# Sixteen frequency groups in place of seventeen, and the loops of two stages written out

## What is computed

```python
def _stu_conv(phi, u, n):            # n = 8192, phi: (sl, 16), u: (b, sl, d)
    Vf = jnp.fft.rfft(phi, n=n, axis=0)
    Uf_p = jnp.fft.rfft(u, n=n, axis=1)
    Uf_m = jnp.fft.rfft(u * sgn3, n=n, axis=1)
    U_plus = irfft(Vf[None, :, :, None] * Uf_p[:, :, None, :], n=n, axis=1)[:, :sl]
    U_minus = irfft(Vf[None, :, :, None] * Uf_m[:, :, None, :], n=n, axis=1)[:, :sl]
    return (U_plus, U_minus * sgn)
...
out = einsum('btkd,k,kde->bte', U_plus, s, Mpp) + einsum('btkd,k,kde->bte', U_minus, s, Mpm)
```

## Time and profile before

| what | value |
|---|---|
| median of 3 runs | 3113.92 us (3101.46 to 3119.89) |
| profiled execution, its own time | 3099.33 us |
| its span, first to last instruction | 3097.6 us |
| TensorE busy / VectorE busy / ScalarE busy | 2450.0 / 1541.0 / 1359.1 us |
| mean granted TensorE clock | 0.897 of full speed |
| `spectrum`: first matmul of line 856 to the first load of `inverse` | 938.4 to 2280.0 us |
| `inverse`: its first to its last matmul | 2286.0 to 2419.7 us |

### The profile page before, as it was taken

How to read it: one execution, slowest core, us unless ns; L and a number is a source line. 1 busy time by engine, 2 the same in 40 slices (tenths; PEclk the granted TensorE clock), 3 DMA queues, 4 the chain that set the end, 5 groups by cost and what they waited for, 6 DMA issues and landing times. The chain is left out here.

```text
span 3097.6 us, 87088 instructions
## 1 busy us (share of the span) xinstructions
PE 2450.0 (79%) x36136; PEld 1874.9 (61%) x36136; DVE 1541.0 (50%) x3563; ACT 1359.1 (44%) x2720; POOL 314.7 (10%) x607
## 2 busy tenths in 40 slices
PE   0455998544609999998999898999979697599998
PEld 0334888522208888888888887888843463144444
DVE  6441343333505656465555555656621165277777
ACT  0562344255006556565656565656621076133332
POOL 0102111100020000000000000000012100122221
PEclk9765899777859999999999999999989698699999
DMA  6437555432461111111111111111048740000000
GB/s 200 128 97 122 104 104 104 118 120 106 139 135 34 43 41 42 42 42 42 42 42 42 42 42 40 44 37 47 22 145 294 260 128 15 12 23 22 23 22 28
DMA packets 189077, 242.74 MB, mean 78 GB/s; under 512 B 36891, under 2 KB 147278, under 8 KB 185146
## 3 DMA queue, kind: packets, MB, share of 16 engines
q1 hardware_dynamic: 154325, 124.05, 15.0%
q0 software_dynamic: 30368, 94.52, 11.3%
q10 hardware_dynamic: 3969, 18.31, 1.5%
HBM read 145.54 MB, written 91.27 MB: 76 GB/s over the span
## 5 line engine op out<-in xcount | busy, mean ns | idle before, releaser
L958 DVE COPY spc_g<-spc_pz 128x512 f32<-128x512 f32 x1088 | 670.4, 683 | 457.3 <-PE spc_pz L856 457.1
L936 ACT ACTIVATE spc_g<-spc_pz 128x512 f32<-128x512 f32 x1088 | 587.6, 610 | 353.4 <-PE spc_pz L856 351.2
L856 PE MATMUL spc_pz<-spc_v,spc_as 108*128 108x128 bf16 x8704 | 604.5, 223 | 46.8 <-issue 32.9
L856 PEld LDWEIGHTS spc_pz<-spc_v,spc_as 108*128 108x128 bf16 x8704 | 519.8, 99 | 141.6 <-issue 51.7
L874 PE MATMUL spc_pz<-spc_g,spc_u 128*20 128x128 f32 x17408 | 499.6, 274 | 27.8 <-DVE spc_g L958 18.3
L874 PEld LDWEIGHTS spc_pz<-spc_g,spc_u 128*20 128x20 f32 x17408 | 479.7, 133 | 56.9 <-ACT spc_g L936 41.3
L841 PE MATMUL spc_pu<-spc_f,spc_s 128*128 128x256 f32 x816 | 223.7, 400 | 71.8 <-DMA spc_s<-s_sf 71.8
L1470 PE MATMUL moe_ex<-moe_ew,moe_d 128*128 128x512 f32 x512 | 249.8, 610 | 33.0 <-DVE moe_yt L1627 32.6
L1627 DVE SCALAR_TENSOR_TENSOR moe_yt<-moe_ex,moe_gb,moe_yt 128x128 f32<-128x128 f32 x768 | 209.6, 344 | 103.3 <-ACT moe_yt L1529 101.0
L505 DVE SCALAR_TENSOR_TENSOR inv_xo<-inv_pa,inv_mask,inv_xo 128x256 f32<-128x256 f32 x256 | 123.6, 484 | 222.3 <-PE inv_pa L463 161.2
L483 ACT ACTIVATE inv_b<-inv_pb 112x1024 f32<-112x1024 f32 x128 | 125.1, 1021 | 222.0 <-PE inv_pb L442 222.0
(11 more groups left out here) (199 smaller groups left out, 2214.7 us busy)
## 6 DMA issues: line engine op xcount, KB each, us to landing
s_yd<-spc_yo SPq DMA_DIRECT2D x136, 160.0 KB
spc_s<-s_sf POOLq DMA_DIRECT2D x36, 512.0 KB, 6.6
ivs_y<-s_yd POOLq DMA_DIRECT2D x34, 512.0 KB, 5.1
s_td<-ivs_to SPq DMA_DIRECT2D x34, 512.0 KB, 4.7
s_sf<-fwd_so ACTq DMA_DIRECT2D x16, 1024.0 KB, 4.7
ln_t<-s_td SPq DMA_DIRECT2D x32, 512.0 KB, 3.7
inv_x<-s_xn SPq DMA_DIRECT2D x88, 112.0 KB
inv_x<-s_xn POOLq DMA_DIRECT2D x88, 112.0 KB, 8.0
```

Of the source, the lines that this page charges most:

```text
L856: m = pe.matmul(pz[:, (p + 2) % 3, e // 4, 2 * FT * (e % 4):2 * FT * (e % 4) + 2 * FT], AS[:, x, 8 * p + e, :], V[:, k, x, :, FT * t:FT * ...
L936: act.activation(g_out(p, 0), g_in(p, 0), ACT.Copy).then_inc(ga, 1)
L958: v.tensor_copy(g_out(p, 1), g_in(p, 1)).then_inc(gd, 1)
```

## The change

NF1 becomes 16. The real group 16 is packed into group 0: group 0 now has f = 32 f2 for f2 below 64 and f = 16 + 32 (f2 - 64) for the others, so that its real input is slot 0 and its "imaginary" one slot 16. The tables `fw` and `fi` have zeros where the two don't mix. The table `fi` gets a fourth slice, as both halves of the output now have weights of their own. Frequency 0 shares its place with frequency 2048, both real numbers; they must not be mixed as a complex product, so VectorE makes a small tile `U0` (memset and four copies of 128x8) at the start of `spectrum`, and `make_y` takes it for that one frequency. The loops of `spectrum` and `inverse` are written out in Python, so no register, no dynamic address and no branch is left in them. The zero rows in DRAM go.

```diff
-NF1, NF2, NA = 17, 128, 16
+NF1, NF2, NA = 16, 128, 16
...
-            for b in range(NB):
-                sp.dma_start(S["SF"][b, 32], zero[:, 0:256]).then_inc(out_done, 16)
-                n += 1
-            sp.dma_start(S["SP"][32], zero[:, 0:2 * KX]).then_inc(out_done, 16)
...
+        def f_loop(body):
+            for f in range(NF1):
+                body(f, f % 2, f == NF1 - 1)
...
-            with sp.Fori(0, NF1 // 2) as i:
-                for k in range(2):
-                    f = 2 * i + k
-
-                    sp.wait_ge(u_done, UB * (f + 1))
-                    load_tokens((f + 2) % NF1, k)
-                    sp.wait_ge(g_done, NPR * NUN * (f + 1))
-                    load_filters((f + 2) % NF1, k)
...
+            for f in range(NF1 - 2):
+                sp.wait_ge(u_done, UB * (f + 1))
+                load_tokens(f + 2, f % 2)
+                sp.wait_ge(g_done, NPR * NUN * (f + 1))
+                load_filters(f + 2, f % 2)
...
+                    if f == 0:
+                        pe.wait_ge(u0_ready, 5)
...
-                                w = U[:, k, s0:s0 + 5, :, FT * t + 4 * g + j].rearrange("d s b -> d (s b)")
+                                w = U[:, k, s0:s0 + 5, :, FT * t + 4 * g + j] if f + t + g + j else U0[:, x, c]
+                                w = w.rearrange("d s b -> d (s b)")
...
-            with pe.Fori(0, NF1 // 2) as i:
-                for k in range(2):
-                    body(2 * i + k, k, i, False)
-            body(NF1 - 1, 0, NF1 // 2, True)
+            f_loop(body)
...
         def _(v):
+            v.memset(U0[:], 0.0).then_inc(u0_ready, 1)
+            v.wait_ge(u0_ready, 1)
+            v.wait_ge(u_ready, UB + 2)
+            for x in range(2):
+                for c in range(2):
+                    s0 = 3 * c + 4 - x
+                    v.tensor_copy(U0[:, x, c, 3 * c:3 * c + 2], U[:, 0, s0:s0 + 2, :, 0]).then_inc(u0_ready, 1)
...
-        F = A.sb("f", [P, 2, 3, P])
+        F = A.sb("f", [P, 2, 4, P])
...
         def f_loop(eng, body):
-            with eng.Fori(0, NF1 // 2) as i:
-                for k in range(2):
-                    body(2 * i + k, k, i)
-            body(NF1 - 1, 0, NF1 // 2)
...
+            for f in range(NF1):
+                body(f, f % 2, f // 2)
...
-                        for part, w in enumerate(((0, 2), (1, 0))[c]):
-                            m = pe.matmul(pt[:, k, c, CH * x:CH * x + CH], F[:, k, w, :], Y[:, k, part, x, :],
+                        for part in range(2):
+                            m = pe.matmul(pt[:, k, c, CH * x:CH * x + CH], F[:, k, 2 * c + part, :], Y[:, k, part, x, :],
```

More of the change, by code:

```diff
@@ L881, in _, with body @@
             pe.wait_ge(as_in, 16 * 12)
-            def body(f, k, i, last):
-                pe.wait_ge(in_v[k], 96 * (f // 2) + 96 if isinstance(f, int) else 96 * i + 96)
+            def body(f, k, last):
+                pe.wait_ge(in_v[k], 96 * (f // 2) + 96)
                 if not last:
-                    pe.wait_ge(in_s[1 - k], 48 * i + 48 + 48 * k)
+                    pe.wait_ge(in_s[1 - k], 48 * ((f + 1) // 2) + 48)
                 for t in range(NTL):
@@ L945, in body @@
                                 act.activation(yo[:, t, 4 * h:4 * h + 4, :].rearrange("p g e -> p (g e)"), y_at(h), ACT.Copy).then_inc(ya, 1)
-            f_loop(act, body)
+            f_loop(body)
         @block.vector
         def _(v):
+            v.memset(U0[:], 0.0).then_inc(u0_ready, 1)
[5 more added lines that the diff above has]
+                    v.tensor_copy(U0[:, x, c, 3 * c:3 * c + 2], U[:, 0, s0:s0 + 2, :, 0]).then_inc(u0_ready, 1)
             def body(f, k, last):
@@ L964, in body @@
                                 v.tensor_tensor(y, y_at(h), y, ALU.add).then_inc(yd, 1)
-            f_loop(v, body)
+            f_loop(body)
         @block.sync
@@ L975, in body @@
                     for j in range(4):
-                        sp.dma_start(one(dst[:, t, j], f), yo[32 * j:32 * j + YR, t]).then_inc(y_out[t], 16)
-            f_loop(sp, body)
+                        sp.dma_start(dst[f, t, j], yo[32 * j:32 * j + YR, t]).then_inc(y_out[t], 16)
+            f_loop(body)
             for t in range(NTL):
@@ L995, in f_loop @@
         def f_loop(eng, body):
-            with eng.Fori(0, NF1 // 2) as i:
-                for k in range(2):
-                    body(2 * i + k, k, i)
-            body(NF1 - 1, 0, NF1 // 2)
-        def at(ap, f):
-            return ap[f] if isinstance(f, int) else ap[bass.ds(f, 1)].rearrange("o p m -> (o p) m")
+            for f in range(NF1):
+                body(f, f % 2, f // 2)
         @block.gpsimd
@@ L1009, in body @@
                     src = S["YD"][:, :, 3 * NB * part:3 * NB * part + 2 * NB].rearrange("f p r e -> f p (r e)")
-                    pool.dma_start(Y[:, k, part].rearrange("p x m -> p (x m)"), at(src, f)).then_inc(loads[k], 16)
-                pool.dma_start(F[:, k].rearrange("p s b -> p (s b)"), at(I["fi"], f)).then_inc(loads[k], 16)
+                    pool.dma_start(Y[:, k, part].rearrange("p x m -> p (x m)"), src[f]).then_inc(loads[k], 16)
+                pool.dma_start(F[:, k].rearrange("p s b -> p (s b)"), I["fi"][f]).then_inc(loads[k], 16)
             f_loop(pool, body)
@@ L1679, in tables @@
         d1[:, k, 1, 1:, k] = -np.sin(th[:, 1:16])
-    b, f2 = np.arange(P), np.arange(NF2)
+    b = np.arange(P)
     fw = np.zeros((NF1, P, 2, 4, NF2))
-    fi = np.zeros((NF1, NF2, 3, P))
+    fi = np.zeros((NF1, NF2, 4, P))
+    f2 = np.arange(NF2)
     for f1 in range(NF1):
         f = f1 + 32 * f2
+        if f1 == 0:
+            f[64:] -= 2048 - 16
         for z in range(2):
@@ L1687, in tables @@
             c, s = np.cos(t), np.sin(t)
-            fw[f1, :, 0, 2 * z:2 * z + 2] = np.stack([c, -s], 1)
-            if f1 not in (0, 16):
+            if f1:
+                fw[f1, :, 0, 2 * z:2 * z + 2] = np.stack([c, -s], 1)
                 fw[f1, :, 1, 2 * z:2 * z + 2] = np.stack([s, c], 1)
+            else:
+                s[:, 0] = -np.cos(np.pi * (b + z))
+                fw[0, :, 0, 2 * z:2 * z + 2, 0:64] = np.stack([c, -s], 1)[:, :, 0:64]
+                fw[0, :, 1, 2 * z:2 * z + 2, 64:] = np.stack([c, -s], 1)[:, :, 64:]
         t = 2 * np.pi * (np.outer(f, b) % 4096) / 4096
-        w = (1.0 if f1 in (0, 16) else 2.0) / 4096
-        fi[f1] = np.stack([np.cos(t), np.sin(t), -np.sin(t)], 1) * w
+        c, s = np.cos(t) * 2 / 4096, np.sin(t) * 2 / 4096
+        if f1:
+            fi[f1] = np.stack([c, -s, s, c], 1)
+        else:
+            c[0], s[0] = 1 / 4096, -np.cos(np.pi * b) / 4096
+            fi[0, 0:64, 0:2] = np.stack([c, -s], 1)[0:64]
+            fi[0, 64:, 2:4] = np.stack([c, -s], 1)[64:]
     d2 = np.zeros((32, 4, NA, 4))
```

29 lines of the change are left out of this document (12 added, 17 removed).

## The result

The changed kernel takes 2962.41 us (median of 4 runs, 2945.99 to 2973.89) against 3107.69 us for the kernel before in the same sessions (4 runs, 3098.66 to 3119.89). The ratio is 0.952, with a 95% interval of 0.9486 to 0.9555: 4.8% faster. The forecast was 2959 us.

The account below looks back on a forecast made before the run. TensorE's pace was taken to bound the mixing, with losses at loop jumps. 138.0 + 6.5 + 3.3 - 0.3 = 147.5 us less than 3099.3 gives 2951.8; half the 14.6 us median offset added gives 2959 us, range 2935 to 2995.

Parts of the forecast that it names:

- One group less and the loops of the mixing: Mixing: a group fewer saves 74.85 us, writing out the loops 63.2; stage from 1340.4 to 1202.4 us, 138.0 less.
- the sign that I gave: Mixing: if the forecast is right, every full group takes within 0.5 us of 74.8.
- The split of the 63.2 us: Mixing loops: 32.9 us are seven waits at jumps, 30.3 the half clock behind each and late matmuls of line 874.
- The branch by row or by rule: TensorE's mixing loop: 5.0 us a jump by the profile, taken over the skill's 108 ns (0.8 us for seven jumps).
- The rival of the clock: Mixing: low clock comes by itself, so only the waits go and 30.3 us come back; 2989 us, chance 0.09.
- The second rival: Mixing: jumps are not the cause, something else such as late instructions holds TensorE back; 3022 us, chance 0.09.
- The slower one: Mixing: written-out instructions no longer come ahead of their use; stage loses 990 us, 3950 us in all, chance 0.02.
- U0: Start of the mixing: VectorE's memset and four small copies delay its first copy of `G`; +0.3 us, at most 2.7.
- Inverse step: Inverse step: one group less is worth 7.8 us, the larger table costs 1.3; 6.5 us less.
- Filters: Filter stage: one of 17 groups less, at 3.3 us each; 3.3 us less.
- Zero rows: Preparation: five stores go from SyncE's list, hidden by its wait for VectorE; no gain.
- The median: Whole time: profiled execution was 14.6 us under the median of the runs; half of that added to the forecast.

Follow-up runs that it names:

- before_shift: The kernel before plus 40 one-column memsets on VectorE, which move its mixing loop by 40 instructions: 3102.05 us, ratio 0.9989 to the kernel before.
- seventeen_tensor_out: The kernel before, 17 groups, with TensorE's loop of the mixing alone written out: 3097.29 us, ratio 0.9952 to the kernel before.
- hold_two: The changed kernel with TensorE held up seven times in the mixing by two small loads, without a jump: 3024.13 us, ratio 0.977 to the kernel before.
- hold_one: The changed kernel with TensorE held up seven times in the mixing by one small load: 2976.05 us, ratio 0.9568 to the kernel before.
- tokens_first: The changed kernel with group 0's token and filter loads issued before the matrices ahead of the mixing: 2966.8 us, ratio 0.9517 to the kernel before.

## Why the prediction was right, and where its reasons were not

*The time.* 2962 us against 2959, inside the range, and faster as forecast. The profiled executions differ by 136.7 us against a sum of 147.5.

*One group less and the loops of the mixing: forecast 138.0 us, measured 130.5.* The stage was to take 15 x 74.85 + 79.6. The last group took its 79.6, but the others 75.35 in place of 74.85, which makes the 7.5 us. I took the pace from groups 0 and 15 alone. In the changed kernel some instructions of TensorE still come late, 7.4 us in eight places:

```profile
PE spc_pz L864 <- issue: 4.1, 6, 1.4
PE spc_pz L843 <- issue: 3.3, 2, 1.8
```

These places recur at the same groups in other kernels with the same TensorE stream: a gap of 1.8, 2.9, 2.6 and 2.0 us behind group 5 in four of them. Why the fetch falls behind there was not tried. The prediction had put such waits at nothing away from a jump. One of the eleven of line 874 stood in group 16 of the kernel before, behind the loop:

```profile
2231.07 2.18 PE L874 MATMUL spc_pz<-spc_g,spc_u 128*20 128x128 f32 x69 [1.01 <-issue]
```

So the sign that I gave, every full group within 0.5 us of 74.8, failed for 5 of the 15 groups (75.7 to 77.2 us). Two readings of mine were loose and nothing hangs on them: the page's clock reads 9 in all of slices 13 to 29, not 7 to 9, and the 1586 of group 15 are its weight loads, of matmuls its row has 1590.

*The split of the 63.2 us.* The 32.9 us of waits stood as read. **The step that failed is the next one**, in which the other 30.3 us were "the half clock behind each, and matmuls of line 874 that come late just ahead of a jump". The first units behind the jumps took 21.2 us over the usual 11.38. With VectorE's loop shifted (before_shift) that was 12.4 us. So by this difference the half clock is worth 12.4, late matmuls 8.5 and VectorE's late instructions 8.8 us, where the prediction had nothing for the last. The line between the first and the last is not sharp: the seven stretches of half clock lasted 57.8 us in all in the kernel before and 37.4 in before_shift, so a part of the 8.8 is clock again. I had read the compare-and-branch records of TensorE and never looked at what came after VectorE's, since they take 60 ns. The sum was right only because the change writes out both loops; for TensorE's alone it would have been 63 us for what turned out to be 5, as seventeen_tensor_out showed.

*The branch by row or by rule.* The row was right for TensorE (5.0 us; medians of 6.3 and 3.8 in the two loops put back), and the estimate of 0.8 us for seven jumps, from the 108 ns of the Trainium skill ("Advanced Engine Details and Errata", Control Flow Timing), was far off. The trace comes near it in the inverse step alone, whose short loop has branch records of 76 to 231 ns.

*The rival of the clock* falls with hold_two: the clock falls behind a stand without a jump, and in the changed kernel no group boundary has a fall behind it. *The second rival*, late instructions that move with the code, has a grain of truth in the 7.5 us. *The slower one* didn't happen.

*U0: forecast +0.3 us.* Each copy of 128x8 took 164 ns, and VectorE's first copy of `G` began as soon as they were done:

```profile
941.63 0.40 DVE L938 COPY spc_u<-spc_u 128x8 f32<-128x8 f32 x4 [79.88 <-ACT spc_u L905]
941.94 2.47 DVE L947 COPY spc_g<-spc_pz 128x512 f32<-128x512 f32 x4
```

The first unit took 11.9 in place of 11.4 us, so 0.5 us.

*Inverse step: forecast 6.5, measured 8.2 us.* The landing of the table grew from 6.6 to 7.0 us in the median, a little over the 0.35 at worst, but the pace stayed: 118.3 / 15 = 7.89 us a group, 126.5 / 16 = 7.91 before. So neither the larger table nor the loop's end shows in the pace, and one group less is nearly the whole gain; the 1.3 us that I took for the table was the term too large.

```profile
2157.80:2276.10 118.30, 108.23 (x240) 45.09 (x240) 18.04 (x15) 15.35 (x15) 22.14 (x42) 0.99 0.88 290
```

*Filters: forecast 3.3, measured 7.1 us.* The mean clock in the stage was 0.84 before and 0.91 after, which I didn't count and the change doesn't explain. *Zero rows*: nothing, as forecast; the involution began at 242.6 us against 243.3.

*The median.* By stages the misses are +7.2 us in the mixing (U0 counted in), -3.8 in the filters, -1.7 in the inverse step and +9.1 in stages that the change leaves alone: +10.8 in all, the 136.7 against 147.5. The 7 us that I added to the sum for the median took up most of it, which is luck: they were meant for the spread between executions, and they covered misses in the mixing and in stages that stay.

## What to carry to other kernels

In these runs a hardware loop cost next to nothing while nothing was fetched anew at its jump, and 3 to 8 us at each taken jump when something was. Look for it at the record behind the branch, on every engine, and not at the branch's own duration, and count the packets of the instruction queues. When two engines stall at the same place, each hides the other: the time goes only when both are cured, so an experiment on one alone (5 and 10 us here) says next to nothing about the pair (58 us). And on TensorE a stall of 2.4 to 8.4 us mostly cost one or two more in clock afterwards.

## What the runs showed that was not expected

*Forty idle instructions were worth 54 us.* VectorE's loop of 314 instructions costs or doesn't by where it lies. A change anywhere ahead of it in VectorE's code, in another stage even, could have moved it in or out of this, and its effect would have been put down to that change.

*Where much of the spread between the traces comes from.* The involution, whose code is the same in all these kernels, took 355.1 us in one, 364.8 before, 371.2 after and 394.7 in another, in step with the mean granted clock of the stage (last columns: clock, DMA share, GB/s; windows of hold_one, before, after and tokens_first):

```profile
243.50:598.60 355.10, 281.34 (x6144) 266.23 (x6144) 124.82 (x260) 124.84 (x128) 70.07 (x121) 0.86 0.60 107
```

```profile
243.30:608.10 364.80, 290.27 (x6144) 274.59 (x6144) 124.94 (x260) 125.14 (x128) 69.89 (x121) 0.83 0.60 104
```

```profile
242.60:613.80 371.20, 297.18 (x6144) 281.15 (x6144) 124.87 (x260) 125.39 (x128) 70.03 (x121) 0.81 0.58 102
```

```profile
242.90:637.60 394.70, 323.73 (x6144) 306.37 (x6144) 124.82 (x260) 126.24 (x128) 70.01 (x121) 0.75 0.54 96
```

These 40 us are more than most effects measured here, which is why the experiments were read by the stage. What decides the clock there was not tried.
